# Exchanging the order of pieces of work on the engines of a software pipeline: four tables of places sought anew, in a two-layer transformer on one core

## What is computed

```python
x = x + _L0_attn_ref(_layernorm(x), ...)   # 16 heads of 8, softmax((q k + q rel_k[idx]) / sqrt(8)), out = attn v + attn rel_v[idx]
x = x + _L0_ffn_ref(_layernorm(x), ...)    # per token: low-rank k, v over the 16 heads, softmax over heads; then 8 experts, dense, by a gate
x = x + _L1_attn_ref(_layernorm(x), ...)   # linear attention, 8 heads of 16, features 1, x, x (x) x / sqrt(2)
x = x + _L1_ffn_ref(_layernorm(x), ...)    # top 2 of 8 experts (hidden width 176) and a shared expert
```

## Time and profile before

| | us |
|---|---|
| median of 3 runs (range) | 740.95 (739.88 to 742.17) |
| the profiled execution | 742.6, of which span 740.8 |
| TensorE busy (weight loads) | 642.9, 87% (514.6) |
| VectorE busy | 546.9, 74% |
| ScalarE busy | 385.0, 52% |
| GpSimd busy | 145.3, 20% |
| mean granted TensorE clock | 0.964 |

### The profile page before, as it was taken

One profiled execution on the slowest core, in us unless ns is written; L12 is line 12 of the kernel. 1 busy time (PEld: TensorE's weight loads), 2 busy tenths in 40 slices (PEclk: granted clock), 3 DMA queues, 4 the chain that ended last, 5 costly groups with the idle time before them and its releaser, 6 DMA issues.

```text
span 740.8 us, 16761 instructions
## 1 busy us (share of the span) xinstructions
PE 642.9 (87%) x6432; PEld 514.6 (69%) x6432; DVE 546.9 (74%) x1337; ACT 385.0 (52%) x907; POOL 145.3 (20%) x178
## 2 busy tenths in 40 slices
PE   2687576987999899999998999989998998778987
PEld 1576455765787688777886688768876886456666
DVE  2432587579778986799678986798679967898375
ACT  3375235456646745665655655575566463413532
POOL 2413201330233023300512023301420012001100
PEclk9799679999899999999999999999999999899999
DMA  5502000200110002000110011000200001000000
GB/s 131 226 2 27 11 1 6 26 9 1 15 16 10 1 8 23 15 2 1 23 16 8 1 23 16 9 1 1 29 11 1 1 9 15 1 1 7 2 8 7
DMA packets 75908, 13.43 MB, mean 18 GB/s; under 512 B 69803, under 2 KB 74933, under 8 KB 75701
## 3 DMA queue, kind: packets, MB, share of 16 engines
q1 hardware_dynamic: 73202, 10.78, 8.1%
q0 software_dynamic: 384, 1.05, 0.5%
q10 hardware_dynamic: 2244, 0.55, 0.3%
HBM read 8.95 MB, written 3.16 MB: 16 GB/s over the span
## 4 chain that ended last, share of the span: by engine, by line
PE 40%; issue 25%; DVE 23%; ACT 4%; POOL 3%; DMA 2%; SPq 1%; ACTq 0%; POOLq 0%; DVEq 0%
PE bank L1140 5%; PE bank L1347 4%; DVE prod L876 4%; DVE lg L882 4%; PE bank L1161 4%; PE bank L1348 3%; PE bank L1179 3%; PE bank L1263 3%; DVE nmx L825 3%; PE bank L1203 3%; PE bank L1374 2%; PE bank L1150 2%; DVE at L907 2%; DVE prod L901 2%; PE bank L1376 2%
## 5 line engine op out<-in xcount | busy, mean ns | idle before, releaser
L540 ACT ACTIVATE pm<-bank,nmx 128x256 f32<-128x256 f32 x256 | 100.5, 480 | 67.9 <-DVE nmx L825 67.7
L825 DVE TENSOR_REDUCE nmx<-bank 128x2 f32<-128x512 f32 x128 | 82.2, 684 | 47.7 <-PE bank L1150 47.3
L548 ACT ACTIVATE pT<-bank 128x512 f32<-128x512 f32 x128 | 76.6, 598 | 69.9 <-PE bank L1161 69.5
L1140 PE MATMUL bank<-kT,qbd 64*64 64x256 f32 x1024 | 87.7, 405 | 10.3 <-POOL qr L650 9.6
L1161 PE MATMUL bank<-w,pm 128*128 128x128 f32 x512 | 82.7, 286 | 13.8 <-ACT pm L540 7.2
L605 ACT ACTIVATE ha<-bank,w 128x256 f32<-128x256 f32 x104 | 49.5, 476 | 66.3 <-PE bank L1348 66.3
L1035 DVE SCALAR_TENSOR_TENSOR hu<-bank,w,ha 128x256 f32<-128x256 f32 x104 | 49.9, 481 | 45.9 <-ACT ha L605 45.8
L1179 PE MATMUL bank<-tv,pT 128*128 128x128 f32 (+1 forms) x512 | 81.8, 280 | 1.5 <-ACT rvs L524 1.1
L1179 PEld LDWEIGHTS bank<-tv,pT 128*128 128x128 f32 x512 | 72.1, 196 | 9.8 <-issue 5.9
L1161 PEld LDWEIGHTS bank<-w,pm 128*128 128x128 f32 x512 | 61.1, 147 | 24.8 <-ACT pm L540 14.3
L1347 PE MATMUL bank<-xfT,w 128*128 128x256 f32 x208 | 66.1, 399 | 3.9 <-DVE hu L1035 3.8
(11 more groups left out here) (203 smaller groups left out, 1281.5 us busy)
## 6 DMA issues: line engine op xcount, KB each, us to landing
w<-wpack_dram SPq DMA_DIRECT2D x1, 3944.0 KB, 12.2
xin<-x_in_dram SPq DMA_DIRECT2D x8, 128.0 KB, 2.1
d_qdh<-qdh SPq DMA_DIRECT2D x8, 128.0 KB, 1.8
d_rv<-rvs SPq DMA_DIRECT2D x64, 16.0 KB, 2.2
out_dram<-xo POOLq DMA_DIRECT2D x8, 128.0 KB, 2.3
qc<-d_qdh SPq DMA_DIRECT2D x15, 64.0 KB, 3.8
tv<-d_ev SPq DMA_DIRECT2D x1, 736.0 KB, 4.7
w<-wpack_dram SPq DMA_DIRECT2D x1, 513.0 KB, 4.3
```

The costliest lines, as they stand in the source:

```text
L540: a = act.activation(pm[:, s % 2, c, j], b_s[c][:, j * S:(j + 1) * S], exp, bias=nmx[:, i:i + 1])
L548: act.activation(view(pT, (c * RTC + 2 * s) * C * P, [[1, 2 * C * P]]), b_t[:], copy).then_inc(pT_ready[0], 1)
L825: v.tensor_reduce(nmx[:, i:i + 2], b_s[c][:].rearrange("p (j k) -> p j k", j=2), AX_X, ALU.max, negate=True).then_inc(max_ready[0], 1)
L1140: mm(b_s[c][cols:cols + P // 2, j * S:(j + 1) * S], qbd[rows:rows + P // 2, i], kT[rows:rows + P // 2, t % 2, u], start=True, stop=False, ...
```

## The change

The tables of places are replaced: all four of `ENGINE_AT` and the three of `MOVED`. Places may now be halves. Nothing else is touched: each engine issues the same instructions with the same operands, banks and waits, in another order. By the sequences that `in_turn` gives, on TensorE 337 of the 744 pieces stand at another position, none more than 11 positions away, and 330 pairs of pieces are exchanged; on ScalarE 240 of 544 (195 pairs, at most 16 positions), on VectorE 143 of 601 (85 pairs, at most 5), on GpSimd 25 of 96 (14 pairs, at most 2). SyncE's program is unchanged.

Around `up` of image 4 TensorE's order becomes: 4 turn1, 2 chunk 9, 5 turn 3, 4 down, 2 chunk 10, **4 up**, 3 sum3, 6 turn0, 5 scores 3, 5 turn 4, 5 relative 1, 2 chunk 11, 3 taylor 0, 5 turn 5, 5 relative 2, 5 relative 3, 3 taylor 1, 2 chunk 12, 3 weigh3 0, 5 turn 6. The same two pieces (`relative` 1 of the next image, `sum3` of the one before) go behind `up` in every period from the `up` of image 2 to that of image 6. Further: on VectorE `scale0` goes ahead of `up` or of `chunk` 10, and `chunk` 8 ahead of `scores` 2, in some periods; on GpSimd `residual` goes ahead of `root1`, and `qkv3` ahead of the addition of `scale1` from image 2 on; on ScalarE `keep3` 1 goes ahead of the exponentials of `scores` 4; on TensorE, for image 0, `relative` 4 goes behind `scores` 4, and `relative` 0 of image 1 ahead of `back` 1; for image 7 `blocks` 0 goes ahead of `store` on GpSimd, and `out3` of image 6 ahead of `mix_scale` on VectorE.

The diff, cut to the start of some tables (all the others are replaced in the same way):

```diff
@@ -111,50 +111,57 @@
-ENGINE_AT = {"PE": [-386, -343, -289, -243, -91, 61, 196, 0, 60, 120, 180, 240, 300, 360, 420, 26, 68, 91, 146, 174, 187, 205,
-                   237, 274, 295, 343, 383, 394, 414, 435, 448, 90, 135, 195, 196, 221, 226, 256, 276, 303, 303, 389, 413, 431,
-                   444, 463, 463, 215, 293, 417, 532, 194, 65, 474, 491, 521, 557, 545, 567, 570, 575, 590, 602, 611, 617, 630,
-                   649, 661, 673, 676, 676, 685, 691, 696, 703, 716, 726, 749, 751, 753, 756, 760, 777, 783, 791, 796, 812, 838,
-                   851, 876, 887, 903, 915, 916, 947, 957, 966, 989, 1006, 1051, 1088, 1116, 1155, 1160, 1170, 1176, 1181, 1190,
-                   1222, 1222, 1236, 1254, 1257, 1268, 1273, 1285, 1341, 1360, 1362, 1377, 1385, 1416, 1432, 1435, 1443, 1459,
-                   1518, 1549, 1585, 1599, 1633, 1646, 1650, 1654, 1666, 1684, 1710, 1726, 1764, 1812, 1826],
...
-MOVED = {0: [-335, -180, -157, -118, -31, 10, 72, 0, 0, 0, 0, 0, 0, 0, 0, 29, 5, 17, 21, 6, 2, 20, 13, 16, 16, 4, -18, 20,
-             13, 4, 10, -14, 1, -24, -8, -13, 27, 6, 6, 28, 29, 12, -7, 3, -3, 6, 6, -10, 21, 5, 3, 40, -80, 1, 9, 20, 6,
-             11, 3, 7, 3, 0, -3, 1, 4, 0, -6, -16, -22, -21, -21, -16, -13, -7, -14, -5, -9, -6, -6, 0, -1, -2, -2, 0, 1,
...
+ENGINE_AT = {"PE": [-445.5, -339, -278, -249.5, -90, 113, 163, 0, 60, 120, 177.5, 241, 302.5, 360, 420, 38.5, 77, 96, 144.5,
+                   179.5, 192.5, 211, 225.5, 268.5, 296, 348.5, 387, 399, 415, 437, 449, 88, 189.5, 196.5, 198, 220.5, 222.5,
+                   253, 275, 329, 339, 390, 402, 432.5, 434.5, 460.5, 463.5, 204, 308, 405, 524, 198, 156, 473, 492, 532, 558,
+                   552, 565, 568, 588, 591, 606.5, 608.5, 616.5, 625.5, 650, 659.5, 660.5, 672, 676, 679, 679, 679, 694.5, 703,
+                   714, 727.5, 740, 764, 765.5, 766.5, 773, 796.5, 799, 817, 828, 838.5, 849.5, 857.5, 892, 902.5, 911, 919.5,
+                   943, 953.5, 962, 995, 1027, 1059, 1090, 1136.5, 1150, 1162, 1168, 1171.5, 1173.5, 1207, 1219, 1219, 1226,
+                   1248, 1257.5, 1287, 1301, 1324, 1349.5, 1360.5, 1367, 1376.5, 1388, 1403.5, 1431, 1435, 1441, 1458.5, 1520,
+                   1550, 1584, 1606.5, 1629.5, 1642.5, 1650, 1659.5, 1674, 1696, 1705, 1732, 1759, 1816, 1838],
...
+             "DVE": [-354.5, -314, -290.5, -188, -88, 87, 141, 0, 60, 120, 178.5, 240, 301.5, 357.5, 420, 43, 65, 90, 131.5, 143,
+                    166, 203, 239, 289, 312, 344, 366.5, 370, 392, 432, 452, 97, 121, 169, 172, 212, 220, 284, 316, 353, 363,
+                    369, 393, 474, 481.5, 491, 493, 204, 332, 395, 545, 106, 103, 443, 457, 502, 539, 536, 549, 562, 577, 583,
+                    600.5, 601.5, 631, 636, 647, 654, 655, 666, 670, 671, 671.5, 671.5, 683.5, 698, 704, 704.5, 705.5, 719,
...
+MOVED = {0: [-488, -493, -365, -195, -212, -252, -189, 0, 0, 0, 0, 0, 0, 0, 0, 9, -11, 5, 12, 10, 10.5, 10, 6, -1, 7, 5,
+             -13, 14, 15, -6, -3, -12, -16, -4, 19, 23, 23, 0, -12, -15, -10, 2, -6, -2, -3, -4, -4, 19, -8, 0, -22, 9,
+             -110, 0, 13, 17, 15, 15, 12, 13, 2, 4, -3, -2.5, -1, 8, 1, -4, -4.5, -15.5, -19.5, -17.5, 16.5, 16.5, 4.5,
...
```

More of the change, by code:

```diff
@@ L113 @@
 ALL_AT = PREPARE_AT + ATTENTION_AT + FEED_AT + SECOND_AT + LATE_AT
-ENGINE_AT = {"PE": [-386, -343, -289, -243, -91, 61, 196, 0, 60, 120, 180, 240, 300, 360, 420, 26, 68, 91, 146, 174, 187, 205,
[6 rows of a table removed]
-             "ACT": [-417, -399, -292, -247, -222, 5, 62, 0, 60, 120, 180, 240, 300, 360, 420, 17, 49, 92, 135, 163, 185, 194,
[6 rows of a table removed]
-             "DVE": [-355, -323, -280, -119, -90, -2, 73, 0, 60, 120, 180, 240, 300, 360, 420, 39, 67, 77, 117, 162, 204, 208,
[6 rows of a table removed]
-             "POOL": [-314, -295, -250, -151, -111, -46, 31, 0, 60, 120, 180, 240, 300, 360, 420, 6, 110, 110, 118, 171, 191, 200,
[6 rows of a table removed]
-MOVED = {0: [-335, -180, -157, -118, -31, 10, 72, 0, 0, 0, 0, 0, 0, 0, 0, 29, 5, 17, 21, 6, 2, 20, 13, 16, 16, 4, -18, 20,
[15 rows of a table removed]
+ENGINE_AT = {"PE": [-445.5, -339, -278, -249.5, -90, 113, 163, 0, 60, 120, 177.5, 241, 302.5, 360, 420, 38.5, 77, 96, 144.5,
[7 rows of a table added]
+             "ACT": [-392.5, -327, -289, -256, -75.5, 57, 229, 0, 60, 120, 177.5, 245, 301.5, 360, 420, 32, 59.5, 101, 150.5, 165,
[7 rows of a table added]
+             "DVE": [-354.5, -314, -290.5, -188, -88, 87, 141, 0, 60, 120, 178.5, 240, 301.5, 357.5, 420, 43, 65, 90, 131.5, 143,
[7 rows of a table added]
+             "POOL": [-315.5, -292, -217.5, -205, -147.5, -27, 38, 0, 60, 120, 178.5, 245, 301.5, 360, 420, 12, 64, 91, 168.5, 181,
[7 rows of a table added]
+MOVED = {0: [-488, -493, -365, -195, -212, -252, -189, 0, 0, 0, 0, 0, 0, 0, 0, 9, -11, 5, 12, 10, 10.5, 10, 6, -1, 7, 5,
[18 rows of a table added]
 PIECES = sorted([(at, k, piece) for k, (piece, at) in enumerate(zip(ALL, ALL_AT))])
```

## The result

The kernel after takes 736.12 us (median of 18 runs, 731.68 to 742.19), the one before 740.92 in as many (737.42 to 747.42): ratio 0.9936, 95% interval 0.9911 to 0.9961, so 4.8 us faster. Forecast were 732.4 and 8.6 us less, range 725 to 740.5. The sign, the range and the stage of most of the gain were right; the gain is little over half of the forecast one.

What follows compares the result with a forecast made beforehand. The middle was taken to be near TensorE's own work, its period a VectorE stretch plus a TensorE stretch. Middle -6.6, fill -3.1 and costs +1.1 gave -8.6 us, so 732.4 us from 740.95; range 725 to 740.5.

Steps and rivals of the forecast that it cites:

- The two stretches: Middle: each image's period is a VectorE stretch (up to join 0) plus a TensorE stretch (join 1 to next up).
- the main term: Middle: relative 1 and sum3 leave the TensorE stretch for behind up, 1.36 us in each of five periods, -6.8 us.
- the 1.5 given back: Middle, at up: idle time for q1 in three images, +0.9, and scale0 delaying up in two, +0.6 us.
- GpSimd's masks: +0.2 for one image: Middle: qkv3's masks under VectorE's last scale1 instruction stretch it, +0.2 us for one image where TensorE has no slack.
- rival 2: Images 2 to 7: GpSimd's masks block VectorE's second scale1 pair, up to 2.0 us each, 744 us in all; chance 0.09.
- (d): Fill, image 1's VectorE stretch: keep3 1 ahead of scores 4's exponentials removes VectorE's wait before scores 5, -0.8 us.
- The single gains of the middle: Middle: scale0 of image 6 ahead of chunk 10, -0.5; chunk 8 ahead of scores 2 and cover for turn_out, -0.8 us.
- Fill: forecast -3.1: Fill: sum of (a) -1.1, (b) -0.5, (c) -0.7 and (d) -0.8 us, bounds 0 and -4.8.
- (a): Fill, image 0: relative 4 behind scores 4 on TensorE removes its 1.10 us wait from the scores chain, -1.1 us.
- (b): Fill: relative 0 of image 1 goes into the 5.1 us wait before back 1, so turn_out comes earlier, -0.5 us.
- (c): Fill: GpSimd's residual of image 1 ahead of root1 no longer stretches VectorE's scale1 of image 0, -0.7 us.
- Costs: Late images: blocks 0 of image 7 under scale2 of image 5, +0.5; out3 ahead of mix_scale in the drain, +0.4 us.

Runs made afterwards that it cites:

- mask_late: The kernel after with GpSimd's masks (qkv3 of images 1 to 6) put back behind its addition of scale1; 733.89 us, ratio 0.9901 to before.
- main_pair: main_only plus ScalarE's read-out of sum3 put behind its chunk 10 in the five periods; 746.29 us, ratio 1.0056 to before.
- after_again: The kernel after unchanged, traced and timed a second time; 734.16 us, ratio 0.9932 to before.
- drain_new: The kernel before with new places only for pieces whose old place is 4000 or behind (the drain); 741.08 us, ratio 0.9995.
- mid_new: The kernel before with new places only for pieces whose old place lies from 1610 to 4000 (the middle); 737.80 us, ratio 0.9959.
- warm_after: The kernel after with 35 unused products of constants ahead of TensorE pieces that wait in the drain; 735.68 us, ratio 0.9939 to before.
- main_only: The kernel before with only relative 1 and sum3 moved behind up on TensorE in the five middle periods; 748.42 us, ratio 1.0107.

## Why the prediction was right and where it failed

**The two stretches held.** VectorE reaches `join` 0 20.0 us behind its first `dot` in both kernels (418.81; 413.18 below), and the whole gain lies behind it: 60.7 to 59.6 us in the period of image 4. `taylor` 1 no longer waits, `join` 1 still does, 0.69 for 1.11. Lines of the kernel after that answer to the earlier trace rows:

```profile
399.56 1.14 PE L1309 MATMUL bank<-q3h,k 64*128 64x256 f32 x8
...
414.35 0.70 PE L1381 MATMUL bank<-w,hu 128*128 128x256 f32 x2 [0.69 <-DVE xo L1062]
...
413.18 0.60 DVE L1062 SCALAR_TENSOR_TENSOR xo<-bank,rw,x 128x128 f32<-128x128 f32 x2
```

**The step that failed is the main term, "-6.8: five times 1.36", less the 1.5 given back.** It took the two pieces to stand "just before `up`", with nothing else that bounds TensorE there. The rows that it went by the earlier trace rows are of image 5, the one period of the five in which `relative` 1 stands behind `turn1`. In the others it stands ahead of `turn1`, while VectorE does `scale1`. TensorE's timeline before, at `up` of image 4: last products of `qkv3`, `relative` 1, `turn1`, `down`, `up`:

```profile
391.05 0.71 PE L1277 MATMUL bank<-w,h3T 128*128 128x128 f32 x4 [0.75 <-ACT k L580]
391.60 0.39 PE L1179 MATMUL bank<-tv,pT 128*128 128x128 f32 x2
...
392.50 0.38 PE L1071 MATMUL bank<-w,hh 128*128 128x128 f32 x2
...
394.11 0.65 PE L1226 MATMUL bank<-hT,w 128*64 128x256 f32 x2
...
396.58 1.10 PE L1234 MATMUL bank<-w,dT 128*128 128x256 f32 x4
```

And the kernel after, without `relative` 1 (its `turn1` is the row at 387.19 under mask_late):

```profile
385.86 0.71 PE L1284 MATMUL bank<-w,h3T 128*128 128x128 f32 x4 [0.75 <-ACT k L587]
...
388.87 0.65 PE L1233 MATMUL bank<-hT,w 128*64 128x256 f32 x2
...
391.33 1.10 PE L1241 MATMUL bank<-w,dT 128*128 128x256 f32 x4 [0.31 <-DVE q L872]
```

From start to start, for the `up` of images 2, 3, 4, 5, 6 (us):

| kernel | `qkv3` to `turn1` | `turn1` to `down` | `down` to `up` |
|---|---|---|---|
| before | 1.44 1.44 1.44 1.01 1.44 | 1.90 2.34 1.61 2.56 1.20 | 2.47 in all |
| after | 1.33 1.33 1.33 1.24 1.20 | 1.67 1.67 1.67 1.23 1.23 | 2.47 in all |
| mask_late | 1.02 1.02 1.02 0.92 0.89 | 1.67 1.67 1.67 1.24 1.23 | 2.47 in all |
| main_pair | 1.01 1.02 1.02 1.02 1.40 | 2.33 2.76 1.89 2.32 1.23 | 2.47 in all |

- `up` follows `down` by 2.47 us with `sum3` between them and without: the way over VectorE's q1 takes that long in all four kernels, and `sum3`'s 0.47 is replaced by waiting. The forecast gave back 0.3 at `up` for three images; all of the 0.47 went, for those three and, with `turn` 3 in its place, for image 6.
- The wait before `turn1` was put at nothing. `relative` 1 hid VectorE's `scale1`; its 0.89 us bring 0.42 with the masks late and 0.11 with them early. Only for image 5, where it stood behind `turn1`, does the period have nearly all of the 1.36 (1.10 from `qkv3` to `up`).
- "GpSimd's masks: +0.2 for one image" was 0.3 in each of the five periods (mask_late): the likeliest case held rival 2's mechanism at a sixth of its price, and it acts in every image.
- The fifth of the five exchanges lies in the period from image 1 to 2, which the sum books under fill (d) as well; see there. The period from image 6 to 7 has none, and brought none: its 75.97 us before hold a spell at half clock, and three traces with the old order have 74.46 to 74.72 there, against 74.35 to 74.51.

By this table the pair is worth about 1.6 us over the five periods with the masks where they are, where 5.3 net were forecast; the four middle periods came down to 79.7 us on average, not to 79.3. The single gains of the middle were right or better, an estimate from the same marks: 0.67 from `turn1` to `down` of image 3, where the 0.46 wait before `chunk` 9 closes, 0.39 behind `up` of image 4, where `scale0` no longer stands, and 0.6 to 0.8 ahead of `qkv3` in the period that has `turn_out`'s wait. No experiment takes one of these alone, and the exchange of `relative` 1 and `sum3` was never undone to its true old place. As for doing it alone, main_pair is the test: 2.8 us longer than before in four periods.

**Fill: forecast -3.1, found -1.0 to -1.7, fifth exchange of the pair included.** The first `dot` of image 0, forecast 2.3 us earlier, shows no gain beyond the spread of one order (94.2 on average with either). (a), -1.1, brought nothing: `relative` 4 is out of the way, and TensorE waits for ScalarE's copy one piece on; there are 0.91 and 0.97 us of waits where there were 0.48 and 1.10; from the first to the last `scores` of image 0 it is 34.70 us after and 34.65 before, and in the pair after_again and drain_new 35.07 and 35.11:

```profile
35.98 0.66 PE L1147 MATMUL bank<-kT,qbd 64*64 64x256 f32 x8 [0.91 <-ACT pm L547]
```

(b), -0.5, was right: from `back` 1 to `turn_out` 2.04 us (75.65 to 77.69) instead of 2.59. (c), -0.7, was right in its own row and wrong in its sum. The pair takes 0.60 and 1.00 instead of 1.15 and 1.18, but `residual` now meets another VectorE instruction, the one-time scaling of weights in `norm1` of image 0. VectorE's timeline before, then after, and GpSimd's after:

```profile
80.84 1.44 DVE L759 TENSOR_SCALAR w<-w 128x128 f32<-128x128 f32 x5
```

```profile
80.45 2.39 DVE L766 TENSOR_SCALAR w<-w 128x128 f32<-128x128 f32 x5
...
80.71 0.77 POOL L664 TENSOR_TENSOR xres<-xin,r 128x256 f32<-128x256 f32 x1 [13.46 <-DVE x L851]
81.44 1.32 POOL L669 TENSOR_TENSOR v<-vraw,r 128x128 f32<-128x128 f32 x2
```

0.73 us won, 0.95 paid. I had looked for a moment in which GpSimd was idle and not asked what VectorE did in it. (d), -0.8, hit its number by the clock and not by the wait. Image 1 to 2 takes 73.78 us in both traces of the kernel after and 74.55 and 74.60 in drain_new and mid_new, with the old fill. But the two old ones have 3.4 us at half clock at 180 to 184 us, and the first two have none; warm_after, the kernel after as far as here, has such a spell at 183 to 186 and takes 74.58, like them. So at like clock the period is the same, as far as these few traces can tell, and (d) and the pair's fifth exchange together didn't shorten it: TensorE's 3.07 us wait is down to 1.47 (before `turn_o3`), but 1.45 and 1.06 stand elsewhere in the period, and all its waits come to 7.6 us for 7.2. VectorE's 1.32 before `scores` 5, the price that (d) went by, is absent in drain_new and mid_new too. What differs is how often the clock falls there: in six of six traces with the old order, for 3.4 to 6.8 us (74.55 to 76.23, and 77.50 in main_only), in one of eight with the new one. Whether that comes of the 3.07 us wait being split wasn't tried alone.

**Costs** of the drain: +0.2, where +0.9 was forecast.

**The clock** was missed as a source of noise. Single executions of one kernel differ by 5 us in fill and drain; the profiled execution of before had some 4 us of it: 2.7 in the fill (237.49 against 234.8) and 1.5 in the period from image 6 to 7. That a total of -4.8 lies in the forecast range owes something to luck: the main term missed by 3.7 and (a) and (c) by 2.0 together, (d) came by way of the clock, and lower costs and larger single gains made up for part of it.

## What to carry to other kernels

A piece taken out of a stretch in which TensorE seems busy throughout is worth its own time only if no operand from another engine becomes the limit in its place. Mark the points at which TensorE takes such an operand, and look at what stands between two marks in every period, not in one: here `down` to `up` was 2.47 us with `sum3` or without, and the earlier trace rows came from the one period of five that was unlike the others. Moving a piece on one engine moves a wait on every engine that reads it: check the readers' orders first (1.1 to 1.5 us a period in main_only). To price an exchange by undoing it, put the pieces back to their true old places, and compare the two sequences. Work put where its own engine is idle may still stretch a neighbour's instruction, so look at what the other one runs in that moment. And where a clock changes between executions, take gains from the stages that repeat to 0.02 us, and use totals only as a check of the sum.

## What the hardware showed that was not expected

- Two executions of one program with the same waits up to 656 us part there: one runs at half clock for 13.7 us, the other doesn't, 5.0 us of difference. Mean granted clock and time go together over the 18 executions of the kernel after (0.98 and 733 us, 0.96 and 740 us).
- A spell of 3.4 us at half clock in the period from image 1 to 2 costs 0.8 us (73.78 and 74.58, one order), in that from image 6 to 7 1.4 to 1.5 (74.35 to 74.51, and 75.89 and 75.91 in mask_late and warm_after).
- VectorE and GpSimd: five `tensor_scalar` of 128x128 take 1.44 us alone and 2.39 beside two GpSimd additions that last 0.77 and 1.32; a pair of them 1.01 beside one addition and 1.32 beside a mask.
